# The second batch's activation blocks, moved out of the first step of attention and made in eight pieces

## The chip, the cores and the metric

The kernel runs on one core of a Trainium2 chip. The core has five engines that run side by side and meet at semaphores: TensorE (matrix products and transposes, PE in the profile), VectorE (DVE), ScalarE (ACT), GpSimd (POOL) and SyncE (SP), which here only issues transfers. Each engine takes its instructions in order. The metric is the time of one execution on the device in microseconds; a comparison goes by the median of several runs.

## The reference, cut to what matters

Two batches of 1024 tokens with 512 features go through a gated linear attention and then a feed-forward layer, each inside `x + layernorm(f(layernorm(x)))`.

```python
def _L0_attn_ref(hidden_states, qkv_w, out_w, gate_w, norm_w):   # 32 heads of 128
    qkv = silu(hidden_states @ qkv_w.T)             # q, k, v of each head
    ...
    # blocks of tokens, in order; kv is the state of a head
    scores = einsum(cq, ck) * diag_decay
    out    = scores @ cv + (cq * q_decay) @ kv
    kv     = kv * block_decay + (ck * k_decay).T @ cv
    ...
    xf = attn * rsqrt(mean(attn * attn) + EPS)
    return (sigmoid(hidden_states @ gate_w.T) * norm_w * xf) @ out_w.T
def _L0_ffn_ref(x, gate_t, up_t, down_t, gate_s, up_s, down_s):  # integer weights with scales
    hidden = silu(x @ gate_w.T) * (x @ up_w.T)
    return hidden @ down_w.T
```

## The kernel before, in words

**Steps.** Attention takes 32 steps: 16 pairs of heads for batch 0 (steps 0 to 15), then the same 16 pairs for batch 1 (16 to 31). The feed-forward layer follows. Step w is written as `first_window` (step 0) or `window(w)` on each engine, and `window(w)` also finishes pair a = w - 1: its attention, its gating and its share of the output projection, which VectorE adds into `y` (`add_out`).

**Products.** In a step the normalised activations are multiplied with the pair's weights of four kinds: k, q, v and the gate (KK, QQ, VV, GG). Each kind is a 2 by 2 block product done as seven products by Strassen's scheme in Winograd's form. The seven activation factors (B_11, B_21, B_22 and the combinations T_1 to T_4) lie in `xb`, seven blocks that stay for a whole batch; the weight factors are made anew for each kind (`combine_weights` on GpSimd). `product(w, kind, i)` is factor product i; I write KK5 for product 5 of kind KK. Every number is split in a high and a low half (`_hi` by ScalarE, `_lo` by a subtraction on GpSimd or VectorE), and a product is six matmuls of 128 x 512. The results are put together on VectorE (`keep_s2`, `keep_s3`, `finish_22`, `finish_12`, `finish_21`) and go through silu or sigmoid on ScalarE (`activate`).

**Attention of a pair.** VectorE turns k in two halves (`turn_k`), SyncE writes it to HBM and reads it back token by token (`k_write`, `k_read`), ScalarE applies the decay (`k_decay`). v goes the same way (`v_write`, `v_read`, then `turn_v`). GpSimd makes `query_decay`. TensorE runs `scores`, `contributions` and `attend`; VectorE runs `decay_scores`, `update_state` and `gate`.

**Both batches' blocks.** `xb` of batch 0 is made before and in step 0. Batch 1's blocks are also made in step 0: SyncE loads segments 2 and 3 of x into `y` (free until step 1), VectorE and ScalarE normalise them, TensorE turns them in eight fills of four transposes (`second_batch_fill`), ScalarE keeps them (`keep_second`), VectorE forms the combinations (`combine_second`), and the seven blocks in two halves each go through a ring of three buffers (`stage_hi`, `stage_lo` in turn on VectorE and GpSimd, `stage_write`) into the HBM tensor `x_blocks`, 14 writes of 512 KB in rows of 2 KB. `stages_out` makes VectorE, ScalarE and GpSimd wait for the last writes, since the buffers lie over tensors that step 1 uses. In step 15 SyncE loads the blocks into `xb`, each behind the last product that reads the old one (`activations`).

**Other work that fills steps.** In steps 2 to 15 ScalarE's queue loads the integer weights 128 x 512 at a time, three a step, into `tile_a`, and VectorE looks for the largest (`look_at_ints`, `look_at_block`). In steps 17 to 25 batch 0's output is normalised and turned for the feed-forward layer, one tile of 128 tokens a step: `load_tile`, `add_tile`, `statistics_of`, `tile_root`, `scales_of`, `normalise_tile`, `turn_tile` (four transposes), `tile_hi`, `tile_lo`, `store_tile`. I call 17 to 25 the tile steps.

The order on VectorE around the place where a piece's work is put, `window(w)`:

```python
gate(a, 0, 1)
if finish is not None:
    tile_lo(finish)
turn_k(w, 1, 0)
turn_k(w, 1, 1)
if checks is not None:
    look_at_block(checks, 0)
update_state(a, 1, 0)
keep_s3(w, QQ)
```

Of the kernel before, what the change touches and what calls it, by code (L numbers as in the profile page):

```python
# [6 lines left out]
P = 128  # L7
# [42 lines left out]
WIDTH_CHECKS = 3 * FF * HID // (P * HID)  # L50
# [68 lines left out]
def sandwich_kernel(nc, x, w_attn, w_out, norm_w, tables, w_ints, ffn_scales, down_s, out):  # L119
    ctx = ExitStack()  # L120
    with ctx:
# [15 lines left out]
        tile_stats = sb("tile_stats", [P, 6])  # L137
        tile_meanvar = sb("tile_meanvar", [P, 2])
        tile_var = sb("tile_var", [P, 1])
        tile_stdev = sb("tile_stdev", [P, 1])  # L140
        tile_rstd = sb("tile_rstd", [P, 1])
        tile_shift = sb("tile_shift", [P, 1])
        rms_term = sb("rms_term", [P, TILES])
        block_max = sb("block_max", [P, CHECKS_PER_WINDOW])
        ints_max = sb("ints_max", [P, CHECKS_PER_WINDOW])
        part_max = sb("part_max", [P, 1])
        all_max = sb("all_max", [P, 1])
# [15 lines left out]
        x_in = [None] + [sem(f"x_in{s}") for s in range(1, NSEG)]  # L163
# [7 lines left out]
        stage_hi_done = sem("stage_hi_done")  # L171
        stage_lo_dve, stage_lo_pool = sem("stage_lo_dve"), sem("stage_lo_pool")
        stage_out = [sem(f"stage_out{j}") for j in range(3)]
# [66 lines left out]
        tile_b = sb("tile_b", [P, HID], scope=two)  # L240
        v_tok = sb("v_tok", [P, QUADS, 2, CH, QUAD], scope=two)
        tile_a = sb("tile_a", [P, HID], scope=two)
# [6 lines left out]
        state = sb("state", [P, 2, CH, HD], scope=two)  # L249
# [10 lines left out]
        check = tile_a[:, :].bitcast(I32)  # L260
# [9 lines left out]
        sb("below_state", [P, 2 * SEQ], scope=one)  # L270
        xf1 = sb("xf1", [P, HALVES, 2, SEG], scope=one)
        tt1 = sb("tt1", [P, 4, SEG], scope=one)
        stage = sb("stage", [P, 3, 2, SEG], F32R, one)
# [37 lines left out]
        w_blocks = w_ints.rearrange("(c p n) -> c p n", p=P, n=HID)  # L311
        x_tiles = x.rearrange("(s t p) h -> s p t h", t=CH, p=P)
        x_rows = x.rearrange("(t p) h -> t p h", p=P)
        out_tiles = out.rearrange("(s t p) h -> s p t h", t=CH, p=P)
# [31 lines left out]
        norm_a = [NSEG + s for s in range(NSEG)]  # L346
        norm_b = [None, None, 2 * NSEG, 2 * NSEG + 1]
        norm_c = [2 * NSEG + 2 + s for s in range(NSEG)]
# [4 lines left out]

        def stages_out(eng):

            for j in range(3):
                eng.wait_ge(stage_out[j], 16 * ((2 * NB - j + 2) // 3))

        @block.sync
        def _(sp):  # L360
# [46 lines left out]
            def activations(b, i):  # L407

                sp.wait_ge(proj_done, products_until(PAIRS - 1, GG, i))
                sp.dma_start(xb[:, b].bitcast(F32), x_blocks[b]).then_inc(xb_in[b], 16)  # L410

            def stage_write(j):

                i, b = j // NB, j % NB
                if j % 2 == 0:
                    sp.wait_ge(stage_lo_dve, j // 2 + 1)
                else:
                    sp.wait_ge(stage_lo_pool, j // 2 + 1)
                sp.dma_start(x_blocks[b, :, :, i], stage[:, j % 3].bitcast(F32)).then_inc(stage_out[j % 3], 16)
# [48 lines left out]
            def first_window():  # L468
                for s in (2, 3):
                    sp.wait_ge(xt_done, BT)  # L470
                    sp.dma_start(y[:, tiles_of(s)], x_tiles[s]).then_inc(x_in[s], 16)
# [6 lines left out]
                for j in range(3):  # L478
                    stage_write(j)
                k_read(0, 0)  # L480
                weights(1, QQ, 1)
                stage_write(3)
                stage_write(4)
                v_write(0, 1)
                v_write(0, 0)
                stage_write(5)
                v_read(0, 0)
                weights(1, VV, 1)
                stage_write(6)
                v_read(0, 1)  # L490
                pair_table(1, 1)
                for j in range(NB, 2 * NB):
                    stage_write(j)
# [4 lines left out]
            sp.dma_start(y[:, tiles_of(1)], x_tiles[1]).then_inc(x_in[1], 16)  # L498
# [58 lines left out]
        def _(pool):  # L557
# [68 lines left out]
            def window(w, first=False, next_weights=True, rms_of=None, tile=None):  # L626
# [40 lines left out]
            def stage_lo(j):  # L667

                b = j % NB
                if b in (B_11, B_21, B_22):  # L670
                    src = xf1[:, int(b == B_22), int(b != B_11)]
                else:
                    src = tt1[:, (T_2, T_3, T_1, T_4).index(b)]
                pool.wait_ge(stage_hi_done, j + 1)
                pool.tensor_tensor(stage[:, j % 3, 1], src, stage[:, j % 3, 0].bitcast(F32),  # L675
                                   ALU.subtract).then_inc(stage_lo_pool, 1)

            def first_window():
# [8 lines left out]
                stage_lo(1)  # L687
                split_lo_s(0, GG)
                split_lo_a(0, GG)
                stage_lo(3)  # L690
                combine_weights(1, KK)
                stage_lo(5)
# [5 lines left out]
                stage_lo(7)  # L698
                stage_lo(9)
                split_lo_s(1, QQ)  # L700
                split_lo_a(1, QQ)
                stage_lo(11)
                stage_lo(13)
                stages_out(pool)
# [50 lines left out]
            window(1, first=True)  # L755
            with pool.Fori(2, PAIRS - 1) as w:
                window(w)
# [64 lines left out]
        def _(act):  # L822
# [43 lines left out]
            def keep_second(f):  # L866

                i, u = f // 4, f % 4
                act.wait_ge(xt_done, BT + f + 1)
                if f == 4:  # L870
                    act.wait_ge(t_done, 2 * 4)
                    act.wait_ge(stage_lo_dve, 4)
                    act.wait_ge(stage_lo_pool, 3)
                act.activation(xf1[:, u // 2, :, (u % 2) * 2 * P:(u % 2 + 1) * 2 * P],
                               yp[f % 2][:, :].rearrange("p (k n) -> p k n", k=2),
                               ACT.Copy).then_inc(xf_done, 1)

            def stage_hi(j):

                i, b = j // NB, j % NB  # L880
                if b in (B_11, B_21, B_22):
                    act.wait_ge(xf_done, BT + 4 * (i + 1))
                    src = xf1[:, int(b == B_22), int(b != B_11)]
                else:
                    act.wait_ge(t_done, 4 * (i + 1) + t_order.index(b) + 1)
                    src = tt1[:, (T_2, T_3, T_1, T_4).index(b)]
                wait(act, stage_out[j % 3], 16 * (j // 3))
                act.activation(stage[:, j % 3, 0], src, ACT.Copy).then_inc(stage_hi_done, 1)

# [20 lines left out]
            def split_out_hi(a):  # L910
                if isinstance(a, int) and a == 0:
                    stages_out(act)
# [55 lines left out]
            def look_at_ints(c):  # L968
                act.wait_ge(max_done, c + 1)
                act.dma_start(check[:, :], w_blocks[c]).then_inc(check_in, 16)  # L970
# [24 lines left out]
            def tile_root(i):  # L995

                act.wait_ge(tile_step, 5 * i + 3)
                act.activation(tile_stdev[:, :], tile_var[:, :], ACT.Sqrt).then_inc(tile_sd_ready, 1)
# [20 lines left out]

            def ffn_convert(n):  # L1020
# [9 lines left out]
            def window(w, next_weights=True, checks=None, first_done=False, finish=None, begin=None,  # L1030
                       into_ffn=False):
# [7 lines left out]
                if finish is not None:  # L1039
                    tile_root(finish)  # L1040
                activate(w, KK, OUT11)
                keep_s1(w, QQ)
                split_out_hi(a)
                if finish is not None:
                    normalise_tile(finish)
                split_hi_s(w, VV)
# [6 lines left out]
                if finish is not None:  # L1053
                    tile_hi(finish)
                square(a, 0, 1)
# [10 lines left out]
                if finish is not None:  # L1066
                    store_tile(finish)
                k_decay(w, 1, 0)
                k_decay(w, 1, 1)
# [11 lines left out]
                if checks is not None:  # L1081
                    look_at_ints(checks + 2)
                if begin is not None:
# [29 lines left out]
            def first_window():  # L1113
# [7 lines left out]
                square_root(2)  # L1121
                normalise(y_tile(2), y_tile(2), 2)
                keep_second(0)
                keep_second(1)
# [4 lines left out]
                square_root(3)  # L1129
                normalise(y_tile(3), y_tile(3), 3)  # L1130
                activate(0, KK, OUT21)
                keep_second(2)
                keep_second(3)
# [3 lines left out]
                stage_hi(0)  # L1137
                stage_hi(1)
                stage_hi(2)
# [6 lines left out]
                stage_hi(3)  # L1146
                activate(0, VV, OUT11)
                stage_hi(4)
                keep_s1(0, GG)
                activate(0, VV, OUT22)  # L1150
                stage_hi(5)
# [6 lines left out]
                stage_hi(6)  # L1158
                keep_second(4)
                keep_second(5)  # L1160
                activate(0, GG, OUT11)
                keep_second(6)
                keep_second(7)
                activate(0, GG, OUT22)
                for j in range(NB, NB + 3):
                    stage_hi(j)
# [1190 lines left out]
```

## Time and profile before

| what | value |
|---|---|
| median of 3 runs | 2441.73 us (2439.56 to 2442.05) |
| profiled execution, its own time | 2444.16 us |
| its span | 2442.4 us |
| TensorE busy, of the span | 2357.6 us (97%) |
| GpSimd busy | 1685.1 us (69%) |
| VectorE busy | 1406.8 us (58%) |
| ScalarE busy | 1190.5 us (49%) |

The span is the time from the first to the last instruction on the core. Busy time counts an engine's own work; an engine that isn't busy waits for another, and the idle time in front of an instruction is given in brackets with what ended it.

### The profile page before, as it was taken

What the parts mean: (1) busy time and instruction counts of PE and PEld (TensorE: products, weight loads), DVE (VectorE), ACT (ScalarE), POOL (GpSimd) and SP (SyncE); (2) the same over time, 40 slices, a digit from 0 to 9 for tenths busy, and PEclk for the clock granted to TensorE, in tenths of its full rate; (3) what the DMA queues carried; (4) which work ended last, traced back from release to release, by engine and by line L of the source; (5) the groups of instructions that cost most, each with busy time, mean ns of one, the idle gap of its engine ahead of it and who ended that gap; (6) DMA issues with size and microseconds to landing.
All of it is one profiled execution on the core that took longest, in us unless ns stands there. A gap on an engine that the chain in (4) does not pass through costs nothing.

```text
span 2442.4 us, 38239 instructions
## 1 busy us (share of the span) xinstructions
PE 2357.6 (97%) x12256; PEld 2011.5 (82%) x12256; DVE 1406.8 (58%) x2479; ACT 1190.5 (49%) x1719; POOL 1685.1 (69%) x1331
## 2 busy tenths in 40 slices
PE   4799999999999999999999999999999999899996
PEld 3588888888888888878888888888888888788885
DVE  5456665666666565656555555555555555465655
ACT  6544444444444444435555444444444444366563
POOL 4567777777777777767777777777777776474674
PEclk7899999999999999999999999999999999999998
DMA  3634444344344443363444444443333334512222
GB/s 108 211 118 125 129 128 122 123 125 125 118 126 129 129 128 122 125 232 116 149 130 129 136 137 137 137 138 126 112 110 110 113 110 139 178 61 70 78 66 90
DMA packets 156936, 304.94 MB, mean 125 GB/s; under 512 B 22464, under 2 KB 88000, under 8 KB 154176
## 3 DMA queue, kind: packets, MB, share of 16 engines
q1 hardware_dynamic: 143856, 279.37, 36.1%
q10 hardware_dynamic: 13008, 24.65, 2.9%
q8 instruction: 41, 0.67, 0.1%
q14 instruction: 31, 0.25, 0.0%
HBM read 216.92 MB, written 87.03 MB: 124 GB/s over the span
## 4 chain that ended last, share of the span: by engine, by line
PE 87%; POOL 3%; DMA 3%; DVE 3%; ACT 2%; issue 1%; SPq 0%; DVEq 0%; ACTq 0%; POOLq 0%
PE proj L1938 53%; PE yp L1938 17%; PE sc L2004 5%; PE sc L1981 4%; PE sc L2007 4%; PE sc L1994 4%; DMA fraw<-w_ints 1%; DMA v_tok<-v_blocks 1%; POOL f_lo L715 1%; DVE stats L1340 1%; DMA nw<-norm_w 0%; DMA fs_stage<-ffn_scales 0%; ACT y L831 0%; POOL stage L675 0%; POOL h_lo L725 0%
## 5 line engine op out<-in xcount | busy, mean ns | idle before, releaser
L1938 PE MATMUL proj<-xb,w_odd 128*128 128x512 f32 x2688 | 709.3, 402 | 17.9 <-POOL w_odd L579 13.0
L1938 PE MATMUL proj<-xb,w_even 128*128 128x512 f32 x2688 | 683.0, 397 | 16.2 <-DMA xb<-x_blocks 3.9
L1938 PEld LDWEIGHTS proj<-xb,w_even 128*128 128x128 f32 x2688 | 499.7, 190 | 118.5 <-issue 8.4
L1938 PEld LDWEIGHTS proj<-xb,w_odd 128*128 128x128 f32 x2688 | 492.7, 190 | 112.9 <-POOL w_odd L579 13.9
L601 POOL TENSOR_TENSOR qd<-q,table 128x512 f32<-128x512 f32 x128 | 164.5, 1298 | 218.2 <-ACT q L947 218.2
L1529 DVE TENSOR_TENSOR g<-sc,g 128x512 f32<-128x512 f32 x128 | 88.5, 691 | 269.6 <-ACT sq L961 269.5
L592 POOL TENSOR_TENSOR ow_lo<-v_tok,ow_hi 128x1024 fp32r<-128x1024 f32 x32 | 76.4, 2388 | 235.7 <-ACT ow_hi L915 235.7
L1536 DVE TENSOR_TENSOR y<-yp,y 128x512 f32<-128x512 f32 x240 | 164.6, 686 | 109.3 <-PE yp L1938 108.1
L1938 PE MATMUL proj<-x_t,f_hi 128*128 128x512 f32 x896 | 213.8, 391 | 2.5 <-issue 2.5
L586 POOL TENSOR_TENSOR w_odd<-ws,w_odd 128x1024 fp32r<-128x1024 f32 x64 | 153.6, 2400 | 73.6 <-ACT w_odd L907 73.6
L1938 PE MATMUL yp<-ow_hi,g_hi 128*128 128x512 f32 x512 | 202.5, 395 | 0.2 <-DVE y L1536 0.2
L1938 PEld LDWEIGHTS proj<-x_t,f_hi 128*128 128x128 f32 x896 | 168.9, 189 | 37.8 <-issue 2.6
L1938 PE MATMUL yp<-ow_hi,g_lo 128*128 128x512 f32 x512 | 199.5, 390 | 0.0
L1938 PE MATMUL yp<-ow_lo,g_hi 128*128 128x512 f32 x512 | 199.4, 389 | 0.0
L2004 PE MATMUL sc<-pd,v 128*128 128x128 f32 x1024 | 188.4, 276 | 3.3 <-DVE state L1521 3.3
L2007 PE MATMUL sc<-qd,state 128*128 128x128 f32 x896 | 174.1, 276 | 0.0
L2004 PEld LDWEIGHTS sc<-pd,v 128*128 128x128 f32 x1024 | 160.9, 193 | 13.8 <-issue 3.7
L617 POOL TENSOR_TENSOR g_lo<-g,g_hi 128x512 fp32r<-128x512 f32 x128 | 163.4, 1299 | 9.5 <-ACT g_hi L966 9.5
L586 POOL TENSOR_TENSOR w_even<-ws,w_even 128x1024 fp32r<-128x1024 f32 x64 | 153.7, 2401 | 16.9 <-ACT w_even L907 16.9
L613 POOL TENSOR_TENSOR sumsq<-sumsq,sq 128x512 f32<-128x512 f32 x124 | 160.9, 1297 | 4.7
L725 POOL TENSOR_TENSOR h_lo<-hid,h_hi 128x512 fp32r<-128x512 f32 x56 | 73.2, 1309 | 118.7 <-ACT h_hi L1239 118.7
L954 ACT ACTIVATE kd<-k_tok,table 128x512 f32<-128x512 f32 x128 | 85.5, 715 | 128.9 <-DMA k_tok<-k_blocks 128.9
(169 smaller groups left out, 4411.3 us busy)
## 6 DMA issues: line engine op xcount, KB each, us to landing
raw<-w_attn SPq DMA_DIRECT2D x128, 512.0 KB, 3.7
k_blocks<-pd SPq DMA_DIRECT2D x64, 512.0 KB, 3.6
k_tok<-k_blocks SPq DMA_DIRECT2D x256, 128.0 KB, 2.9
v_blocks<-vf SPq DMA_DIRECT2D x64, 512.0 KB, 2.7
v_tok<-v_blocks SPq DMA_DIRECT2D x256, 128.0 KB, 3.0
v_tok<-w_out SPq DMA_DIRECT2D x32, 512.0 KB, 4.5
fraw<-w_ints SPq DMA_DIRECT2D x13, 1024.0 KB, 5.0
tile_a<-w_ints ACTq DMA_DIRECT2D x42, 256.0 KB, 3.5
```

The costliest lines, as they stand in the source:

```text
L586: pool.tensor_tensor(w_lo[slot][:, S_1:S_4 + 1], ws[:, :, :, :], w_hi[slot][:, S_1:S_4 + 1].bitcast(F32), ALU.subtract).then_inc(wlo_s_don ...
L601: pool.tensor_tensor(qd[:, s, h].rearrange("p (c n) -> p c n", c=CH), q[:, h, half(s)].rearrange("p (c n) -> p c n", c=CH), decay.unsqueez ...
L613: pool.tensor_tensor(total, total, sq[:, h], ALU.add).then_inc(ss_done, 1)
L617: pool.tensor_tensor(g_lo[:, h], g[:, h, half(s)], g_hi[:, h].bitcast(F32), ALU.subtract).then_inc(glo_done, 1)
L954: act.activation(kd[:, s, h].rearrange("p c (i d) -> p i c d", i=QUADS), k_tok[:, :, h], ACT.Copy, scale=table[:, TAB_K + h:TAB_K + h + 1] ...
L1529: dve.tensor_tensor(at, sc[h][:, :], at, ALU.mult).then_inc(gated_done, 1)
L1536: dve.tensor_tensor(y[:, t], yp[t % 2][:, :], y[:, t], ALU.add).then_inc(yacc_done, 1)
L1938: last = pe.matmul(psum, s, m, start=start and n == 0, stop=n == len(terms) - 1, skip_group_check=more)
L1981: last = pe.matmul(sc[h][:, chunk(c)], k[:, h, tok], q[:, h, tok], start=True, stop=True)
L1994: last = pe.matmul(sc[h][:, chunk(c)], kd[:, s, h, c], v[:, s, c, h], start=True, stop=True)
L2004: last = pe.matmul(sc[h][:, chunk(c)], v[:, s, c, h], pd[:, s, h, c], start=True, stop=not inter)
L2007: last = pe.matmul(sc[h][:, chunk(c)], state[:, h, (c - 1) % CH], qd[:, s, h, chunk(c)], start=False, stop=True)
```

## The change

Batch 1's blocks leave step 0 altogether: the loads, statistics, fills, `combine_second`, `stage_hi`, `stage_lo`, `stage_write` and `stages_out` are gone. Instead a piece of 2 x 128 tokens and half of the features is made in each of steps 1 to 8. At the end of step w - 1 ScalarE's queue loads two tiles of x (`load_piece`) and VectorE takes their statistics. In step w they are normalised, turned by four transposes, combined by four subtractions of 128 columns, split, and both halves are written to `x_blocks` from ScalarE's queue, 448 KB each in rows of 512 bytes. The buffer `piece` lies where no other tensor does, so `state` moves in SBUF. The tiles are loaded and normalised twice, once for either half of the features. The looks at the integer weights become 21 of 128 x 1024, in steps 9 to 15, and use the same buffer.

In `window(w)` ScalarE has `piece_root` behind `keep_s1(w, KK)`, `normalise_piece` behind `split_out_hi(a)`, `keep_piece` behind `activate(w, KK, OUT21)`, `piece_high` ahead of `k_decay(w, 1, 0)` and `store_high` behind it, and `store_low` and the next `load_piece` behind `gated_hi(a, 1, 1)`. VectorE has `scales_of_piece` behind `update_state(a, 0, 1)`. The diff, cut:

```diff
-WIDTH_CHECKS = 3 * FF * HID // (P * HID)
+WIDTH_CHECKS = 3 * FF * HID // (2 * P * HID)
...
+        piece = sb("piece", [P, 2 * NB * P], scope=two)
...
+        tiles = piece[:, 0:2 * HID].rearrange("p (t n) -> p t n", t=2)
+        piece_hi = piece[:, 0:NB * P].bitcast(F32R)
+        piece_lo = piece[:, NB * P:2 * NB * P]
+        mix = piece_lo.rearrange("p (b n) -> p b n", b=NB)
...
@@ GpSimd, window @@
                 add_squares(a, 1, 0, first)
+                if part is not None:
+                    split_piece(part)
...
+            def split_piece(j):
+                pool.wait_ge(piece_hi_done, j + 1)
+                pool.tensor_tensor(piece_lo.bitcast(F32R), piece_lo, piece_hi.bitcast(F32),
+                                   ALU.subtract).then_inc(piece_lo_done, 1)
...
@@ ScalarE @@
+            def load_piece(j, u):
+                wait(act, piece_hi_out, 16 * j)
+                for s in range(HALVES):
+                    act.dma_start(tiles[:, s], x_pairs[u, HALVES + s]).then_inc(piece_in[s], 16)
+            def piece_root(j):
+                act.wait_ge(piece_step, 7 * j + 5)
+                act.activation(tile_stdev[:, :], tile_var[:, :], ACT.Sqrt).then_inc(piece_sd_ready, 1)
+            def normalise_piece(j):
+                act.wait_ge(piece_step, 7 * j + 7)
+                for s in range(HALVES):
+                    act.activation(tiles[:, s], tiles[:, s], ACT.Identity, bias=tile_shift[:, s:s + 1],
+                                   scale=tile_rstd[:, s:s + 1]).then_inc(piece_normed, 1)
+            def keep_piece(j):
+                act.wait_ge(piece_turned, j + 1)
+                wait(act, piece_lo_out, 16 * j)
+                for m in range(2):
+                    act.activation(mix[:, B_21 * m:B_21 * m + T_3 + 1:T_3],
+                                   yp[0][:, 2 * P * m:2 * P * (m + 1)].rearrange("p (s n) -> p s n", s=HALVES),
+                                   ACT.Copy).then_inc(piece_kept, 1)
+            def piece_high(j):
+                act.wait_ge(piece_mixed, 4 * (j + 1))
+                act.activation(piece_hi, piece_lo, ACT.Copy).then_inc(piece_hi_done, 1)
...
@@ VectorE @@
+            def statistics_of_piece(j, n):
+                for s in range(HALVES):
+                    dve.wait_ge(piece_in[s], 16 * (j + 1))
+                    dve.bn_stats(tile_stats[:, s], tiles[:, s]).then_inc(piece_step, 1)
+                dve.wait_ge(piece_step, 7 * j + 2)
+                keep_b(n)
+                for s in range(HALVES):
+                    dve.bn_aggr(tile_meanvar[:, s], tile_stats[:, s]).then_inc(piece_step, 1)
...
+            def mix_piece(j):
+                dve.wait_ge(piece_kept, 2 * (j + 1))
+                dve.tensor_tensor(mix[:, T_1], mix[:, T_3], mix[:, B_11], ALU.subtract).then_inc(piece_mixed, 1)
+                dve.wait_ge(piece_mixed, 4 * j + 1)
+                dve.tensor_tensor(mix[:, T_2], mix[:, B_22], mix[:, T_1], ALU.subtract).then_inc(piece_mixed, 1)
+                dve.tensor_tensor(mix[:, T_3], mix[:, B_22], mix[:, T_3], ALU.subtract).then_inc(piece_mixed, 1)
+                dve.wait_ge(piece_mixed, 4 * j + 2)
+                dve.tensor_tensor(mix[:, T_4], mix[:, B_21], mix[:, T_2], ALU.subtract).then_inc(piece_mixed, 1)
...
@@ VectorE, window @@
                 gate(a, 0, 1)
                 if finish is not None:
                     tile_lo(finish)
+                if part is not None:
+                    mix_piece(part)
                 turn_k(w, 1, 0)
...
                     statistics_of(begin, w)
+                elif next_part:
+                    statistics_of_piece(w, w)
...
@@ VectorE, first_window @@
-                combine_second(0)
-                stage_lo(0)
...
                 turn_v(0, 1, 0)
                 turn_v(0, 1, 1)
-                stage_lo(10)
-                stage_lo(12)
+                statistics_of_piece(0, 0)
...
@@ TensorE, window, behind product(w, KK, 4) @@
+                if part is not None:
+                    turn_piece(a, part, a)
...
@@ TensorE, project_out(a, 0) @@
+                    if part is not None:
+                        pe.wait_ge(piece_kept, 2 * (a + 1))
```

## Rows read from the trace of the kernel before

**Rows 1.** The page's forty slices: TensorE's granted clock, in tenths.

```profile
PEclk7899999999999999999999999999999999999998
```

**Rows 2.** Stretches in us: busy time (count) of each engine, clock, DMA share, GB/s.

```profile
100.00:120.00 20.00, 12.35 (x51) 9.78 (x49) 13.89 (x18) 7.58 (x13) 9.96 (x7) 0.83 0.72 223
...
200.00:260.00 60.00, 60.00 (x322) 51.57 (x322) 37.51 (x65) 26.95 (x40) 42.79 (x36) 1.00 0.43 132
...
633.30:695.90 62.60, 62.60 (x337) 53.90 (x336) 38.23 (x67) 29.01 (x44) 45.48 (x37) 1.00 0.39 126
```

**Rows 3.** Timeline, TensorE, step 0 and the start of step 1.

```profile
44.51 2.90 PE L1938 MATMUL proj<-xb,w_even 128*128 128x512 f32 x6 [3.69 <-DVE k L1442]
...
85.26 2.93 PE L1938 MATMUL proj<-xb,w_odd 128*128 128x512 f32 x6 [6.37 <-POOL w_odd L579]
...
106.68 5.49 PE L1938 MATMUL proj<-xb,w_odd 128*128 128x512 f32 x12 [4.85 <-DVE g L1448]
111.96 2.97 PE L1938 MATMUL proj<-xb,w_even 128*128 128x512 f32 x12
...
131.35 1.06 PE L2004 MATMUL sc<-pd,v 128*128 128x128 f32 x4
```

**Rows 4.** Timeline, the other engines, step 0.

```profile
76.70 0.61 ACT L947 ACTIVATE q<-q 128x512 f32<-128x512 f32 x1
...
79.87 1.28 POOL L675 TENSOR_TENSOR stage<-tt,stage 128x512 fp32r<-128x512 f32 x1
...
93.27 0.61 ACT L947 ACTIVATE vf<-vf 128x512 f32<-128x512 f32 x1
...
101.61 1.30 DVE L1490 STREAM_TRANSPOSE v<-v_tok 128x512 f32<-128x512 f32 x2 [3.88 <-DMA v_tok<-v_blocks]
...
102.84 0.65 DVE L1388 TENSOR_TENSOR tt<-xf 128x512 f32<-128x512 f32 x1
...
105.94 0.68 DVE L1448 TENSOR_TENSOR g<-proj,g 128x512 f32<-128x512 f32 x1
```

**Rows 5.** The page's DMA issues: count, KB each, median us to landing.

```profile
k_blocks<-pd SPq DMA_DIRECT2D x64, 512.0 KB, 3.6
...
tile_a<-w_ints ACTq DMA_DIRECT2D x42, 256.0 KB, 3.5
```

**Rows 6.** One tile, ow_hi on ScalarE: once a step; steps 2 and 14.

```profile
L915 ACT ACTIVATE ow_hi<-v_tok x1: 1049/1049/1049, 193.9 to 193.9; 128x1024 fp32r<-128x1024 f32 x1
...
L915 ACT ACTIVATE ow_hi<-v_tok x1: 1049/1049/1049, 945.9 to 945.9; 128x1024 fp32r<-128x1024 f32 x1
```

**Rows 7.** One tile, tile_b on TensorE: ns min/median/max, first and last start.

```profile
L2117 PE MATMUL yp<-ident,tile_b x32: 272/272/273, 1211.2 to 1653.5; 128*128 128x128 f32 x32
```

**Rows 8.** Timeline, four engines, step 19, a tile step.

```profile
1271.71 0.80 ACT L1003 ACTIVATE tile_b<-tile_a,tile_shift,tile_rstd 128x512 f32<-128x512 f32 x1
...
1278.71 0.69 DVE L1529 TENSOR_TENSOR g<-sc,g 128x512 f32<-128x512 f32 x1 [1.53 <-ACT sq L961]
...
1279.92 1.29 DVE L1482 STREAM_TRANSPOSE pd<-k 128x512 f32<-128x512 f32 x2
1281.50 1.11 DVE L1521 SCALAR_TENSOR_TENSOR state<-state,b_prev,sc 128x128 f32<-128x128 f32 x3 [0.28 <-PE sc L1994]
1282.79 0.69 DVE L1448 TENSOR_TENSOR q<-proj,q 128x512 f32<-128x512 f32 x1 [0.18 <-PE proj L1938]
...
1280.15 1.28 POOL L617 TENSOR_TENSOR g_lo<-g,g_hi 128x512 fp32r<-128x512 f32 x1 [0.32 <-ACT g_hi L966]
...
1284.56 1.64 PE L1938 MATMUL proj<-xb,w_odd 128*128 128x512 f32 x6
```

**Rows 9.** One tile (ints_max on VectorE), then timelines around 673 us.

```profile
L1544 DVE TENSOR_TENSOR ints_max<-ints_max,block_max x42: 159/298/1889, 203.8 to 1049.5; 128x1 f32<-128x1 f32 x42
...
672.69 2.41 POOL L586 TENSOR_TENSOR w_even<-ws,w_even 128x1024 fp32r<-128x1024 f32 x1
...
673.40 1.72 DVE L1544 TENSOR_TENSOR ints_max<-ints_max,block_max 128x1 f32<-128x1 f32 x1
```

More of the change, by code:

```diff
@@ L162, in sandwich_kernel @@
         x_first_in = [sem(f"x_first_in{t}") for t in range(CH)]
-        x_in = [None] + [sem(f"x_in{s}") for s in range(1, NSEG)]
+        x_in = sem("x_in")
         const_done, ln_own = sem("const_done"), sem("ln_own")
@@ L239, in sandwich_kernel @@
         k_tok = sb("k_tok", [P, QUADS, 2, CH, QUAD], scope=two)
[L240 removed]
         v_tok = sb("v_tok", [P, QUADS, 2, CH, QUAD], scope=two)
[L242 removed]
+        state = sb("state", [P, 2, CH, HD], scope=two)
         q = sb("q", [P, 2, SEQ], scope=two)
@@ L624, in add_tile, with window @@
                 pool.tensor_tensor(tile_a[:, :], tile_a[:, :], tile_b[:, :], ALU.add).then_inc(tile_added, 1)
-            def window(w, first=False, next_weights=True, rms_of=None, tile=None):
+            def window(w, first=False, next_weights=True, rms_of=None, tile=None, part=None):
                 a = w - 1
@@ L754, in _ @@
             first_window()
-            window(1, first=True)
-            with pool.Fori(2, PAIRS - 1) as w:
+            window(1, first=True, part=0)
+            with pool.Fori(2, 2 * CH + 1) as w:
+                window(w, part=w - 1)
+            with pool.Fori(2 * CH + 1, PAIRS - 1) as w:
                 window(w)
@@ L1067, in window @@
                     store_tile(finish)
+                if part is not None:
+                    piece_high(part)
                 k_decay(w, 1, 0)
+                if part is not None:
+                    store_high(part)
                 k_decay(w, 1, 1)
@@ L1082, in window @@
                     look_at_ints(checks + 2)
+                if part is not None:
+                    store_low(part)
+                if next_part is not None:
+                    load_piece(w, next_part)
                 if begin is not None:
@@ L1170, in first_window @@
                 activate(0, GG, OUT21)
-                for j in range(NB + 3, 2 * NB):
-                    stage_hi(j)
+                load_piece(0, 0)
             square_root(0)
@@ L1510, in update_state @@
                 if s == 0 and h == 0:
-                    if isinstance(a, int) and a == 0:
-                        stages_out(dve)
                     dve.wait_ge(b_kept, a + 1)
@@ L1603, in window @@
                     scales_of(finish)
+                if part is not None:
+                    scales_of_piece(part)
                 keep_s3(w, KK)
@@ L1613, in window @@
                     tile_lo(finish)
+                if part is not None:
+                    mix_piece(part)
                 turn_k(w, 1, 0)
@@ L2009, in attend, with project_out @@
                 last.then_inc(attn_done, 1)
-            def project_out(a, t, tile=None, downs=0):
+            def project_out(a, t, tile=None, downs=0, part=None):
                 if t == 0:
@@ L2015, in project_out @@
                         pe.wait_ge(tile_lo_done, tile + 1)
+                    if part is not None:
+                        pe.wait_ge(piece_kept, 2 * (a + 1))
                 if t % CH == 0:
@@ L2118, in turn_tile, with turn_piece, window @@
                 last.then_inc(tile_turned, 1)
-            def window(w, x_wait=False, rms_of=None, tile=None):
+            def turn_piece(a, i, j):
+                pe.wait_ge(piece_normed, 2 * (j + 1))
+                wait(pe, yacc_done, BT * a - 1)
+                for m in range(2):
+                    for s in range(HALVES):
+                        last = pe.transpose(yp[0][:, chunk(2 * m + s)], tiles[:, s, chunk(2 * m + i)],
+                                            ident[:, :])
+                last.then_inc(piece_turned, 1)
+            def window(w, x_wait=False, rms_of=None, tile=None, part=None):
                 a = w - 1
@@ L2136, in window @@
                     turn_tile(a, tile)
+                if part is not None:
+                    turn_piece(a, part, a)
                 product(w, QQ, 6)
@@ L2147, in window @@
                     pe.wait_ge(rms_ready, rms_of + 1)
-                project_out(a, 0, tile)
+                project_out(a, 0, tile, part=part)
                 product(w, QQ, 4)
```

254 lines of the change are left out of this document (82 added, 172 removed).

## Prediction

> **What bounds the kernel now.** I read the page's forty slices first: TensorE's granted clock is below nine tenths only in the first two and the last of them [rows 1]. The stretches then split the run in two. From 200 us on TensorE is busy 60.00 of 60 us at full clock; from 100 to 120 us it is busy 12.35 of 20 [rows 2]. So a step is bound by TensorE everywhere except at the start, and this change touches both kinds of place: it takes work out of step 0, where TensorE waits for others, and puts it into steps 1 to 8, where TensorE waits for nobody. The profiled execution took 2444.16 us, 1.76 us more than its span; the median of the runs is 2.43 us below it, so I work out differences and subtract them from 2441.73.
>
> **The saving in step 0.** I rebuild the chain of step 0 without the removed work and ask when TensorE would start `attend(0, 0, 0)`, which it now does at 131.35 us [rows 3]. Up to the product KK5 at 44.51 us nothing changes.
> - KK5 takes about 2.8 us at the lower clock. `keep_s3` (0.7) then frees KK3 at 48.0; it also runs at the lower clock and ends near 50.7. Eight more products at 1.38 us each (a pair takes 2.97 with overlap [rows 3]) bring 61.7. Fills and normalisations between them are gone. `finish_12` of QQ stands behind `turn_k(0, 0)`, which waits for the landing of `k_write(0, 1)`; that write is now queued behind the load of step 1's KK weights, released near 56.1. Issue at 56.6 plus 3.6 to 4.5 (median landing 3.6 [rows 5]) plus two transposes gives 63.0 for VV7, a wait of 1.3. ScalarE's last silu of QQ then starts near 65.3.
> - From that silu (76.70) to GG1 (85.26) takes 8.56 now, through GpSimd's two query decays, one `stage_lo` of 1.2 us and two weight splits [rows 3, 4]. Without the `stage_lo` it is 7.3: GG1 at 72.6. TensorE is done at 67.1 and idles 5.5 us; GpSimd, not the activation work, sets this stretch.
> - GG1 to the last silu of VV: 8.0 (85.26 to 93.27), kept: 80.6. From there to `turn_v` 8.34 (93.27 to 101.61), the round trip of v through HBM, kept: 89.0. `turn_v` to GG3 is 5.07 (101.61 to 106.68), of which the four additions of `combine_second` from 102.84 to `decay_scores` take 2.5; 2.6 stay: GG3 at 91.6. From GG3 to KK1 of step 1 is 5.28 (106.68 to 111.96): 96.9. Step 1 starts 15.1 us earlier.
> - From KK1 to `attend(0, 0, 0)` takes 19.4 now, with waits in it (KK2, KK3) that come from `stages_out` and the late `stage_hi`. Run without waits it is seven products and two contributions, 11.3. New in front of it: `statistics_of_piece(0)` makes VectorE wait for two loads that ScalarE issues at about 98.0 and 98.4 (landing 3.5 later, as loads of the same size do [rows 5]). Statistics end near 103.3, `keep_s2` at 104, the two state updates, `scales_of_piece` and `keep_s3` at 107.8, so KK3 waits about 1.1: `attend` at 109.7 with some slow clock.
>
> Saving: 131.35 - 109.7 = 21.7 us. Bounds: three waits stay (1.3, 5.5 and about 4.3 before GG3), and each may cost the clock again (2.90 for six products after one, 5.49 for twelve after another, against 2.97 for twelve). If the cold stretches add up, 18; if v's round trip shortens without the 14 `stage_write`s, 25.
>
> **The cost of a piece, TensorE.** Four transposes a step. Batch 1's tile steps have the same four: their marks lie 442.3 us apart over seven steps and three transposes of 0.11 [rows 7], 63.13 a step, against (945.9 - 193.9) / 12 = 62.67 for batch 0's steps [rows 6]. So 0.46 each, 8 x 0.46 = 3.7 us.
>
> **The cost of a piece, VectorE's queue.** This is the disputed term. I lay the piece over the tile step around 1280 us [rows 8]. ScalarE's normalisation is two activations instead of one, 0.7 more, so `gate(a, 0, 1)` moves from 1278.71 to about 1279.6 and is out at 1280.2. There `mix_piece` takes the place of `tile_lo`. Behind it in the same queue stand two transposes, three state updates and `keep_s3`, from 1279.92 to 1281.50 to 1282.79: at least 3.06 us of work once `mix_piece` is out, and product QQ3 (1284.56) waits for the last. So `mix_piece` may end at 1281.5 without any cost. Its four subtractions of 128 columns are about 0.28 each (between 0.16 for one column [rows 9] and 0.65 for 512 [rows 4]), 1.0 in all: 1281.2, just in time.
>
> But they read two operands from SBUF, and such an operation doesn't run beside GpSimd's. The third look of a check step adds one column to another; the fastest of its kind takes 0.159 us, this one runs from 673.40 to 675.12, which is where GpSimd's split from 672.69 ends [rows 9]. In the piece step GpSimd is at `gated_lo(a, 0, 0)` when the mix begins, and takes `gated_lo(a, 0, 1)` (1.28 us [rows 8]) 0.8 us after the gate, amid the four. The dependent steps of the mix leave it a gap. One such block: the mix ends at 1282.7, QQ3 waits 1.2. Two: 1284.0 and 2.5. None: 0. I take one, since the request falls between the second and third subtraction: 8 x 1.2 = 9.6 us.
>
> The Trainium skill's "SBUF — State Buffer", section "Who interferes with whom", says that an operation with two SBUF inputs contends with a reading GpSimd operation and that whoever comes first has the shared pair for the whole instruction. By that rule all four could be blocked in the worst case, 4 x 1.28 = 5.1 us a step, 41 us in all; the rows here show the block for a single operation and not who wins when both wait. This rule speaks against the change more than anything else I found.
>
> **The rest.** `statistics_of_piece` is 0.7 longer than the tile's; `turn_v` behind it still waits for its load. `split_piece` (896 columns, about 2.1 us on GpSimd by 2.41 for 1024 [rows 9]) delays the low halves that `project_out(4)` and `keep_s1(GG)` want; GpSimd is idle for 17.1 of 62.6 us of a step [rows 2], and what is late there I take as covered. `piece_high` and `store_high` lie in ScalarE's wait for k. The writes go out in 512-byte runs; no row of this kernel prices them alone, so between nothing and 0.5 a step, taken as nothing because the DMA engines are busy 0.39 of a step [rows 2]. The looks at the integers become 21 of 1024 columns in steps 9 to 15 instead of 42 of 512 in 2 to 15: 0.6 longer each; the first one of a step stands in front of QQ3 with about 0.7 of room after a block, so 0 to 0.5 x 7, taken as 0.3 in all. The change of batch (step 16) isn't touched.
>
> **Sum.** -21.7 + 3.7 + 9.6 + 0.3 = -8.1 us: 2433.6 us.
>
> **Rivals.**
> - No block in the mix: -21.7 + 3.7 = -18.0, 2423.7 us. For: there are 1.3 us of room and 1.0 of work. Against: the row at 673.40 and GpSimd's place. Chance 0.30.
> - Two blocks: +20 instead of +9.6, 2444.0 us, no change that can be told. Chance 0.16.
> - Slower: three blocks, 3.8 us before QQ3 in each of eight steps, 30.4 + 3.7 - 21.7 = +12.4, 2454 us. It decides from 2.25 us a step on (18.0 / 8); over 2.9 it is slower by more than 0.2%. For: VectorE and GpSimd alternate if both always have a request. Against: GpSimd is between two operations when the mix starts. Chance 0.12.
> - Step 0 doesn't shorten as said, since its two long waits are GpSimd's splits and v's round trip and neither is removed: if only half is saved (11), the result is +2.6, 2444 us. Against: `stage_lo`, `combine_second` and `stages_out` stand on the chain themselves. Chance 0.07.
>
> **How the numbers follow.** About 0.2% (4.9 us) is what a measurement of this kernel can tell from no change. The forecast has 0.35, with its own range 2428 to 2438. Faster: 0.35 + 0.30 + a little of the last = 0.67. Same: 0.16 + the rest of the last and some overlap = 0.20. Slower 0.13. The range takes in no block with a good step 0 (-21.7) and two blocks with a little more (+4.3): 2420 to 2446.
>
> **What would show it.** In the trace after: `attend(0, 0, 0)` near 110 us (18 to 25 earlier); GG1 still waits for GpSimd, GG3 for VectorE; steps of batch 0 with a piece 64.3 us apart by the mark of `ow_hi` (63.1 if the mix isn't blocked, 65.6 if blocked twice), with TensorE's idle time before the product that follows `keep_s3` of q; some of the mix's subtractions near 1.3 us instead of 0.28; steps 9 to 15 at 62.7. I am wrong if piece steps wait elsewhere (k's round trip, a GpSimd half) or if steps 9 to 15 lengthen.

## The result, and the profile after

The kernel after takes 2446.71 us (median of 20 runs, 2441.72 to 2450.3) against 2442.41 us for the kernel before on the same chips (20 runs, 2439.56 to 2448.47). The ratio is 1.0016 (95% interval 1.001 to 1.0022): 4.3 us slower where the forecast was 8.1 us faster. That is inside the 0.2% which counts as no change, and 0.7 us above the upper end of the range (2446). The profiled execution took 2447.89 us with a span of 2445.7 us.

TensorE's timeline of the kernel after, step 0 and the start of step 1:

```profile
45.26 2.90 PE L1932 MATMUL proj<-xb,w_even 128*128 128x512 f32 x6 [4.17 <-DVE k L1412]
...
64.87 4.42 PE L1932 MATMUL proj<-xb,w_even 128*128 128x512 f32 x18 [1.10 <-DVE q L1433]
...
74.40 2.93 PE L1932 MATMUL proj<-xb,w_odd 128*128 128x512 f32 x6 [5.11 <-POOL w_odd L562]
...
92.89 5.43 PE L1932 MATMUL proj<-xb,w_odd 128*128 128x512 f32 x12 [3.57 <-DVE g L1418]
98.16 2.92 PE L1932 MATMUL proj<-xb,w_even 128*128 128x512 f32 x12
...
108.73 1.65 PE L1932 MATMUL proj<-xb,w_even 128*128 128x512 f32 x6 [0.39 <-DVE k L1418]
110.22 0.61 PE L1998 MATMUL sc<-pd,v 128*128 128x128 f32 x4
```

The products are those of [rows 3]: GG1 comes at 74.40 instead of 85.26, GG3 at 92.89 instead of 106.68, `attend(0, 0, 0)` of step 1 at 110.22 instead of 131.35. Up to `attend`, 21.1 us are gained, and the same two waits stay, for GpSimd's weight split and for VectorE's g. So the loss is behind this point. Stretches between the marks of `ow_hi` (start of one to start of the next; its length, TensorE busy and its count, granted clock, DMA share, GB/s), steps 1, 2, 5 and 7, and the first one without a piece:

```profile
111.39:176.43 65.04, 62.75 (x332) 1.00 0.41 132
176.43:243.29 66.86, 64.45 (x339) 0.97 0.40 128
...
374.24:440.95 66.71, 64.21 (x343) 1.00 0.40 128
...
506.35:571.89 65.54, 63.52 (x343) 1.00 0.40 130
...
636.91:699.58 62.67, 62.67 (x338) 1.00 0.43 139
```

Steps without a piece stay at the 62.67 us of [rows 6]. The eight with one take (636.91 - 111.39) / 8 = 65.69 us, almost the 65.6 that the prediction gave for a mix that is blocked twice. TensorE, which waited for nobody in these steps before [rows 2], now isn't busy for about 2.2 us of each. Its waits from 105 to 640 us (total, times, longest):

```profile
PE proj L1932 <- DVE q L1418: 16.5, 8, 2.5
PE proj L1932 <- DVE k L1418: 0.9, 2, 0.5
PE proj L1932 <- ACT g L879: 0.3, 1, 0.3
PE yp L2100 <- ACT piece L984: 0.2, 1, 0.2
```

The first line is the product that the prediction named: QQ3 waits for `keep_s3` of q in every piece step. Step 7, timelines of VectorE, GpSimd and TensorE, which answer to [rows 8]:

```profile
515.08 0.69 DVE L1497 TENSOR_TENSOR g<-sc,g 128x512 f32<-128x512 f32 x1 [2.30 <-ACT sq L909]
515.69 0.62 DVE L1582 TENSOR_TENSOR piece<-piece 128x128 f32<-128x128 f32 x1
516.34 0.29 DVE L1584 TENSOR_TENSOR piece<-piece 128x128 f32<-128x128 f32 x1
516.55 1.41 DVE L1585 TENSOR_TENSOR piece<-piece 128x128 f32<-128x128 f32 x1
517.88 1.37 DVE L1587 TENSOR_TENSOR piece<-piece 128x128 f32<-128x128 f32 x1
519.17 1.29 DVE L1452 STREAM_TRANSPOSE pd<-k 128x512 f32<-128x512 f32 x2
520.40 1.06 DVE L1489 SCALAR_TENSOR_TENSOR state<-state,b_prev,sc 128x128 f32<-128x128 f32 x3
521.38 0.68 DVE L1418 TENSOR_TENSOR q<-proj,q 128x512 f32<-128x512 f32 x1
...
514.86 1.29 POOL L600 TENSOR_TENSOR g_lo<-g,g_hi 128x512 fp32r<-128x512 f32 x1
516.51 1.29 POOL L600 TENSOR_TENSOR g_lo<-g,g_hi 128x512 fp32r<-128x512 f32 x1 [0.36 <-ACT g_hi L914]
517.76 2.75 POOL L596 TENSOR_TENSOR sumsq<-sumsq,sq 128x512 f32<-128x512 f32 x2
...
522.12 1.65 PE L1932 MATMUL proj<-xb,w_odd 128*128 128x512 f32 x6 [2.02 <-DVE q L1418]
```

Read the ends against each other. The first subtraction ends at 516.31, 0.16 behind GpSimd's first `g_lo` (516.15): it lost 0.33. The third is handed over at 516.55, 0.04 behind the start of the second `g_lo`, and ends at 517.96, 0.16 behind that one's end. GpSimd's `add_squares` follows at once, and the fourth ends at 519.25, 0.12 behind the middle of the two (517.76 + 2.75 / 2). The mix lasts 3.5 us (515.69 to 519.25); the prediction had 1.0 for it without a block and 2.5 with one. The other piece steps show the same four lengths, except that the fourth subtraction of step 1 took 0.69 us.

### The profile page after: what moved, and what is told of

Its sections match the earlier page's. It is cut to its first block, busy times and chain, and to the rows that moved or that the text cites. A ratio compares the mean times of both kernels' runs of the same rounds, so it can differ in the third digit from the quotient of the medians.

```text
span 2445.7 us, 38159 instructions
## 1 busy us (share of the span) xinstructions
PE 2356.5 (96%) x12256; PEld 2010.1 (82%) x12256; DVE 1407.2 (58%) x2488; ACT 1199.5 (49%) x1739; POOL 1691.5 (69%) x1332
## 4 chain that ended last, share of the span: by engine, by line
PE 82%; DMA 5%; DVE 5%; ACT 3%; issue 3%; POOL 1%; SPq 1%; DVEq 0%; ACTq 0%; POOLq 0%
PE proj L1932 50%; PE yp L1932 17%; PE sc L1975 4%; PE sc L1998 4%; PE sc L2001 4%; PE sc L1988 3%; DMA nw<-norm_w 2%; DMA v_tok<-v_blocks 1%; SPq L405 1%; DVE v L1460 1%; DVE pd L1452 0%; ACT k L895 0%; DMA k_blocks<-pd 0%; DMA k_tok<-k_blocks 0%; DVE piece L1587 0%
## 5 line engine op out<-in xcount | busy, mean ns | idle before, releaser
L1932 PE MATMUL proj<-xb,w_odd 128*128 128x512 f32 x2688 | 709.6, 402 | 32.7 <-DVE q L1418 16.5
L1489 DVE SCALAR_TENSOR_TENSOR state<-state,b_prev,sc 128x128 f32<-128x128 f32 x384 | 131.7, 343 | 21.2 <-PE sc L1988 9.8
```

What stands on the lines that cost most here:

```text
L1489: dve.scalar_tensor_tensor(state[:, h, c], state[:, h, (c - 1) % CH], b_prev[:, h:h + 1], new, ALU.mult, ALU.add).then_inc(state_done, 1)
L1932: last = pe.matmul(psum, s, m, start=start and n == 0, stop=n == len(terms) - 1, skip_group_check=more)
```

## The experiments

The first four start from the kernel after, the last four from the second of them ("One operand from PSUM"). Kernels of one group ran beside the same runs of before (2442.43 us for the first group, 2442.7 us for the second).

**Move the mix.** `mix_piece` goes from in front of `turn_k(w, 1, 0)` to behind `keep_s3(w, QQ)`:

```diff
-                if part is not None:
-                    mix_piece(part)
                 turn_k(w, 1, 0)
...
                 keep_s3(w, QQ)
+                if part is not None:
+                    mix_piece(part)
                 turn_k(w, 0, 0)
```

> Change: mix_piece(part) stands behind keep_s3(w, QQ) in VectorE's queue instead of in front of turn_k(w, 1, 0); all else as after. Theory A (what the piece costs is mostly that two of the four subtractions are blocked by GpSimd, so that the mix takes 3.5 us where 1.3 are free before product QQ3): QQ3's wait of 2.0 to 2.3 us a step goes, marks of ow_hi in piece steps 63.3 to 64.0 us apart instead of 65.8, time 2429.5 us (2427 to 2433), ratio to before 0.993 to 0.996. Rival B (the queue is late already when the mix begins, through the statistics before turn_v and the second normalising activation): QQ3 still waits 1 us or more, marks 64.8 or more apart, 2438 to 2443. Rival C (the stall is only moved, to finish_22 and turn_k(0, 0) behind the mix): QQ3 doesn't wait, but a later product does, 2436 to 2446.

Measured: 2427.08 us (5 runs, 2425.0 to 2430.11), ratio 0.9943 (0.9929 to 0.9957). The waits of TensorE from 105 to 640 us:

```profile
PE proj L1932 <- DVE q L1426: 2.3, 7, 0.6
PE yp L2100 <- ACT piece L984: 0.2, 1, 0.2
```

The 16.5 us are gone, and only 2.3 us come back at the next product that waits for q. Blocks still lengthen the subtractions in this place, three of the four; VectorE's timeline in step 7:

```profile
500.25 0.69 DVE L1418 TENSOR_TENSOR q<-proj,q 128x512 f32<-128x512 f32 x1 [0.19 <-PE proj L1932]
500.86 0.28 DVE L1582 TENSOR_TENSOR piece<-piece 128x128 f32<-128x128 f32 x1
501.18 1.33 DVE L1584 TENSOR_TENSOR piece<-piece 128x128 f32<-128x128 f32 x1
502.44 0.82 DVE L1585 TENSOR_TENSOR piece<-piece 128x128 f32<-128x128 f32 x1
503.18 0.82 DVE L1587 TENSOR_TENSOR piece<-piece 128x128 f32<-128x128 f32 x1
503.92 0.70 DVE L1452 STREAM_TRANSPOSE pd<-k 128x512 f32<-128x512 f32 x1
```

The mix takes 3.1 us here, but it now lies where VectorE would wait for k's round trip. Theory A holds; rival B (the queue is late anyway) doesn't, and rival C is worth the 2.3 us. The marks are 63.3 to 63.8 apart.

**One operand from PSUM.** The transposes' bank holds the same numbers as the copy in SBUF, so each subtraction takes its first operand from there:

```diff
-dve.tensor_tensor(mix[:, T_1], mix[:, T_3], mix[:, B_11], ALU.subtract)
+dve.tensor_tensor(mix[:, T_1], yp[0][:, P:2 * P], mix[:, B_11], ALU.subtract)
...
-dve.tensor_tensor(mix[:, T_4], mix[:, B_21], mix[:, T_2], ALU.subtract)
+dve.tensor_tensor(mix[:, T_4], yp[0][:, 2 * P:3 * P], mix[:, T_2], ALU.subtract)
...
-                        pe.wait_ge(piece_kept, 2 * (a + 1))
+                        pe.wait_ge(piece_mixed, 4 * (a + 1))
```

> Change: each of the four subtractions reads its first operand from the transposes' bank yp[0] instead of from the copy in SBUF, so that it has one SBUF input; same place, same count, same semaphores, and project_out(0) waits for the mix instead of for the copy. Theory A (lock): each subtraction takes 0.25 to 0.4 us, none over 0.7; the mix is out about 1.3 us after the gate; QQ3 waits 0 to 0.3; marks 63.3 to 64.0 apart; 2429.5 us (2426 to 2433). Rival D (the mix costs by its work and its chained semaphores, not by the lock): the mix still takes 2.5 us or more, QQ3 waits 1.2 or more, 2440 to 2447.

Measured: 2424.45 us (5 runs, 2422.56 to 2426.47), ratio 0.9926 (0.9913 to 0.994). VectorE's timeline in step 5:

```profile
371.79 0.69 DVE L1497 TENSOR_TENSOR g<-sc,g 128x512 f32<-128x512 f32 x1 [2.31 <-ACT sq L909]
372.40 0.28 DVE L1582 TENSOR_TENSOR piece<-yp,piece 128x128 f32<-128x128 f32 x1
372.71 0.29 DVE L1584 TENSOR_TENSOR piece<-yp,piece 128x128 f32<-128x128 f32 x1
372.92 0.28 DVE L1585 TENSOR_TENSOR piece<-yp,piece 128x128 f32<-128x128 f32 x1
373.12 0.28 DVE L1587 TENSOR_TENSOR piece<-yp,piece 128x128 f32<-128x128 f32 x1
...
375.52 0.68 DVE L1418 TENSOR_TENSOR q<-proj,q 128x512 f32<-128x512 f32 x1
```

Same place, same count, same chain of semaphores on VectorE, and the mix takes 1.0 us instead of 3.5; QQ3 no longer waits. What differs for the subtractions is the memory of one operand, so the block needs the second operand in SBUF. The time is 18.0 us under the kernel before and below the range that I had expected (2426 to 2433). It has the lowest median here, but its interval overlaps those of the moved mix, of both repairs together and of the doubled stores. The forecast for a mix without a block was 18.0 us as well; that it fits to the tenth is luck, since at the mark of step 9 the lead is 15.8 us (616.80 against 632.59) and the rest comes later.

**GpSimd yields once.**

```diff
                 gated_lo(a, 0, 1)
+                if part is not None:
+                    pool.wait_ge(piece_mixed, 4 * (part + 1))
                 add_squares(a, 0, 0, first)
```

> Change: GpSimd waits for the fourth subtraction before add_squares(a, 0, 0), one wait more in its queue; nothing else. Theory A (the third subtraction is blocked by the second gated_lo, the fourth by add_squares): the third stays at 1.4 us, the fourth falls from 1.37 to 0.29; QQ3 waits 1.0 to 1.3 instead of 2.0 to 2.3; marks 64.7 apart; 2438 us (2436 to 2441). That is the single block that the prediction had. Rival D (work, not the lock): no change, 2445 to 2448. A rival to both: GpSimd, later by 0.5 us, delays w_lo or g_lo and TensorE waits there; over 2448.

Measured: 2436.51 us (11 runs, 2431.79 to 2440.1), ratio 0.9977 (0.9968 to 0.9986). TensorE's wait for q, then VectorE and GpSimd in step 2:

```profile
PE proj L1934 <- DVE q L1420: 9.8, 8, 1.6
```

```profile
185.68 0.60 DVE L1584 TENSOR_TENSOR piece<-piece 128x128 f32<-128x128 f32 x1
186.32 0.29 DVE L1586 TENSOR_TENSOR piece<-piece 128x128 f32<-128x128 f32 x1
186.53 0.28 DVE L1587 TENSOR_TENSOR piece<-piece 128x128 f32<-128x128 f32 x1
186.73 1.38 DVE L1589 TENSOR_TENSOR piece<-piece 128x128 f32<-128x128 f32 x1
...
186.51 1.46 POOL L600 TENSOR_TENSOR g_lo<-g,g_hi 128x512 fp32r<-128x512 f32 x1 [0.37 <-ACT g_hi L916]
```

With one long block instead of two the wait is 9.8 us for the eight steps, close to what the prediction reckoned (9.6; in single steps it is 0.87 to 1.58). The time is then 5.9 us under the kernel before, inside the range of the forecast (2428 to 2438) but short of its 8.1. I had expected the block always at the third subtraction. In steps 2 and 7 the third went ahead (0.28, and `g_lo` took 1.46 instead of 1.29), and the fourth was blocked instead: 1.38. The mean of the third is 1.13, of the fourth 0.56. It is one long block in either case.

**Statistics later.**

```diff
-                elif next_part:
-                    statistics_of_piece(w, w)
...
                 turn_v(w, 0, 1)
+                if next_part:
+                    statistics_of_piece(w, w)
```

> Change: statistics_of_piece(w, w), with its keep_b, stands behind turn_v(w, 0, 1) and not before turn_v(w, 0, 0). Theory A: the late output weights move ScalarE's ow_hi by no more than 0.2 us, since it stands behind keep_s1 of q there, and QQ3's wait stays at 2.0 or more; 2443.5 to 2447. Rival B (the queue is late through the statistics): v_tok and the output weights come some 2 us earlier, the mix begins 0.5 us or more earlier, QQ3's wait falls by as much, 2439 to 2443.

Measured: 2444.73 us (11 runs, 2441.73 to 2447.38), ratio 1.0005 (0.9996 to 1.0014). QQ3 waits 14.6 us in all instead of 16.5, and the waits for k are gone. That lies between the two expectations: QQ3's wait fell by 0.24 us a step, where rival B wanted 0.5. From `attend(0, 0, 0)` to the mark of step 9 this trace takes 525.0 us, the one of the kernel after 526.7. So the waits show a small part of the late queue in the loss, not the main one; the times don't show it, since the intervals of the two kernels overlap.

**Both repairs together.** The second and fourth edit in one kernel.

> Change: the subtractions with a PSUM operand and the statistics behind turn_v, both together. If the small waits for keep_s3 of k (0.8 us in two steps) come from the statistics in front of turn_v: they go, 2422.5 us (2421 to 2424.5), 1 to 3 us under the kernel with the PSUM operands alone. Rival: the two edits overlap and nothing is left to gain, 2424.5.

Measured: 2426.42 us (6 runs, 2423.52 to 2428.74), ratio 0.9933 (0.9921 to 0.9945): not better than the PSUM operands alone, whose interval it overlaps, and not the 2422.5 that I had hoped for. The waits for k that VectorE released are gone, but near the end of step 5 TensorE now waits 0.9 us for ScalarE's k; what makes it wait in just that step stays open.

**Transposes twice.**

```diff
-                for m in range(2):
+                for m in (0, 1, 0, 1):
```

> Change: to the kernel with the PSUM operands, each of the four transposes is made twice (eight a step). If TensorE's queue is the bound in the piece steps and a transpose costs 0.115 us there: 8 x 0.46 = 3.7 us more, 2428.2 us (2426.5 to 2430), marks 0.46 further apart. If the transposes lie in time that TensorE has to spare, or cost by their latency (0.60 us for the four in the record): 2424.5, or 2430 and more.

Measured: 2428.37 us (5 runs, 2427.44 to 2429.34), ratio 0.9942 (0.9929 to 0.9955), 3.9 us more than with four. The intervals overlap a little, and the kernel with doubled stores, which ran beside this one, is only 2.4 us faster. The marks are the better evidence: without steps 1 and 5 they are 63.4 to 63.6 apart (63.53 in the mean) against 62.8 to 63.2 (63.00), 0.5 more for four more transposes, which agrees with the 0.46 of the prediction. Over all eight steps the difference is smaller, 1.9 us from `attend(0, 0, 0)` to the mark of step 9, since step 5, with its wait for k, is longer with four than with eight (64.75 against 63.69).

**A long mix without a lock.** Twelve more subtractions in front of the four:

```diff
+                for n in range(12):
+                    if n == 6:
+                        dve.wait_ge(extra, 12 * j + 6)
+                    dve.tensor_tensor(piece[:, (n % 6) * P:(n % 6 + 1) * P], yp[0][:, P:2 * P], mix[:, B_11],
+                                      ALU.subtract).then_inc(extra, 1)
```

> Change: to the kernel with the PSUM operands, twelve more subtractions of the same form (one PSUM, one SBUF operand, 128 columns) in front of the four; they write where the high part goes later. No lock is involved, and the mix gets about as long as in the changed kernel: 0.95 + 12 x 0.21 = 3.5 us. If all of the changed kernel's loss is the length of the mix (its wait before QQ3 and what the clock takes after such a wait): QQ3 waits 1.9 to 2.1 us in each of eight steps, 2446 us (2442 to 2449). If a part of the 22 us between the two kernels is what the lock does to GpSimd: QQ3 waits the same, but the time is 2424.5 + 15 to 16 = 2440 us (2438 to 2442).

Measured: 2447.5 us (11 runs, 2444.65 to 2450.26), ratio 1.0023 (1.0015 to 1.0032). VectorE in step 7, then TensorE's wait:

```profile
515.84 2.59 DVE L1586 TENSOR_TENSOR piece<-yp,piece 128x128 f32<-128x128 f32 x12
518.35 0.28 DVE L1588 TENSOR_TENSOR piece<-yp,piece 128x128 f32<-128x128 f32 x1
...
519.07 0.28 DVE L1593 TENSOR_TENSOR piece<-yp,piece 128x128 f32<-128x128 f32 x1
```

```profile
PE proj L1938 <- DVE q L1419: 16.1, 8, 2.6
```

A mix of 3.5 us made of short, free operations gives the wait of the kernel after (16.1 and 16.5 us) and its time (ratios 1.0023 and 1.0016 to the kernel before, with overlapping intervals). So what the blocks cost is the length that they give to the mix in that place; a further cost, through GpSimd's side, doesn't show.

**Stores twice.** Both stores of a piece are issued a second time, to a spare tensor:

```diff
+                act.dma_start(spare[0, j], piece_hi.bitcast(F32).rearrange("p (b n) -> p b n", b=NB)).then_inc(piece_hi_twice, 16)
                 act.dma_start(piece_blocks[0, j],
...
+                act.dma_start(spare[1, j], mix[:, :, :]).then_inc(piece_lo_twice, 16)
                 act.dma_start(piece_blocks[1, j], mix[:, :, :]).then_inc(piece_lo_out, 16)
```

> Change: to the kernel with the PSUM operands, each store of a piece (high and low part, 128 partitions, 512-byte runs) is issued a second time, to a spare tensor. If the stores are hidden, as the prediction took: 2424.5 us (2423 to 2426). If they are not: up to 0.5 us a step, 2428.5.

Measured: 2425.97 us (5 runs, 2423.04 to 2427.56), ratio 0.9931 (0.9918 to 0.9944). The DMA share of a piece step rises from 0.42 to 0.48, and the time doesn't move by more than the intervals. Its mark of step 9 stands at 616.89 against 616.80. The stores are hidden.

## Why the prediction was wrong

- **The saving in step 0: right.** Forecast 21.7 us, measured 21.1 (131.35 to 110.22). The intermediate points came 0.5 to 1.9 us later than forecast: VV7 at 64.87 (63.0), GG1 at 74.40 (72.6), GG3 at 92.89 (91.6), KK1 at 98.16 (96.9), `attend` at 110.22 (109.7). The rival that step 0 doesn't shorten is out. That the total is so close is in part luck: `attend` starts at 109.4 to 112.1 us in eight of the nine traces with pieces and at 105.60 in the ninth, with the moved mix, whose edit doesn't touch step 0. There GG3 and its neighbour ran at full clock (granted 1.00, 3.01 us for the twelve matmuls), here at the lower level (0.52, 5.43 us), behind waits of nearly the same length (3.46 and 3.57 us).
- **The transposes: right** as far as the runs tell. 3.7 us were forecast; doubling them added 0.5 us to a quiet step, 3.9 us to the median.
- **The mix: this step failed.** Mechanism, place and product were right (`mix_piece` blocked by GpSimd, QQ3 waits for `keep_s3` of q). The sum took one block of 1.2 us a step, 9.6 us; the trace shows two long ones and a third of 0.33 us, and the wait is 16.5 us, 2.06 a step. The room in front of QQ3 was as forecast, some 1.4 us (1.3); the length of the mix was not, 3.5 us (2.5). The prediction laid only `gated_lo(a, 0, 1)` over the mix. It left out what stands behind that in GpSimd's queue: `add_squares(a, 0, 0)`, which starts the moment `gated_lo` is done, and also the end of `gated_lo(a, 0, 0)`, which cost the first subtraction its 0.33. The prediction's argument against more blocks, that GpSimd is between two operations when the mix starts, goes against its own reading two paragraphs earlier and against the trace: `gated_lo(a, 0, 0)` runs until 0.46 us after that start. With `add_squares` held back, the wait was the forecast one (9.8 us). The rival with two blocks (2444.0 us, chance 0.16) is what happened; it gave their wait as 20 us, the wait was 16.5. That 65.69 us a step came so close to its 65.6 is partly luck: the wait was 0.4 shorter, and other terms made up for it.
- **What follows a wait: left out.** From `attend(0, 0, 0)` to the mark of step 9 the kernel before takes 501.2 us (131.35 to 632.59) and the kernel after 526.7 (110.22 to 636.91), 25.5 more. QQ3's waits are 16.5 of it, the transposes 3.7, the small waits for k, g and the piece 1.4 (0.9 + 0.3 + 0.2), and 3.9 are left. Part of that is the clock: behind the wait of step 2, matmuls for `yp` took 0.62 us, though 0.39 is their record at full clock.

```profile
192.20 1.71 PE L1932 MATMUL proj<-xb,w_odd 128*128 128x512 f32 x6 [2.41 <-DVE q L1418]
193.71 0.62 PE L1932 MATMUL yp<-ow_hi,g_hi 128*128 128x512 f32 x1
...
196.26 1.95 PE L1932 MATMUL proj<-xb,w_odd 128*128 128x512 f32 x6
198.05 0.38 PE L1998 MATMUL sc<-pd,v 128*128 128x128 f32 x2
```

  The stretch from 194 to 197, with the same columns as [rows 2]:

```profile
194.00:197.00 3.00, 3.00 (x8) 2.35 (x8) 2.93 (x7) 1.47 (x2) 0.00 (x0) 0.50 0.81 243
```

  That is the lower of the two levels, and it is the only such fall in the piece steps of this trace; it takes away about 1.7 us (3.4 us at half clock). The other 2.2 were not settled. Between kernels that differ in the mix alone, from `attend(0, 0, 0)` to the mark of step 9: with the PSUM operands it takes 506.7 us, with 9.8 us of waits for q (GpSimd yields) 518.3, and with 16.5 us (the kernel after) 526.7. So the waits cost 11.6 and 20.0 us, some 1.2 times their length; the traces of the first two have no fall of the clock there. The long mix without a lock says the same: 16.1 us of waits, 527.0 us, with two falls. In the medians the kernel after is 22.3 us above the one with PSUM operands (2446.71 - 2424.45); what exceeds 20.0 isn't found in the piece steps.
- **Stores, checks, `split_piece`: nothing of them shows.** Stores twice change nothing. The marks of steps 9 to 15 stay 62.7 us apart, so the wider looks are hidden (the sum had 0.3 for them). `split_piece` was not tried alone, but in the piece steps TensorE waits for nothing that GpSimd made.
- **The skill's rule.** The Trainium skill ("SBUF — State Buffer", "Who interferes with whom") says that a VectorE operation with two SBUF inputs contends with a reading GpSimd operation and that the first to come holds the pair of SBUF ports that they share for its whole length. The traces agree: three subtractions of 0.28 us ended 0.12 to 0.16 us behind a GpSimd operation, and with one operand in PSUM none was longer than 0.29. The worst case that the prediction worked out from it, four full blocks, didn't come: the first subtraction met only the last 0.46 us of a GpSimd operation, and the second fell into a gap of 0.36 us. The kernel before had a hint: `tile_lo`, which the mix replaced in the overlay on the tile step, reads one of its operands from `yp`, and it takes 0.68 us every time, so its place said nothing on two SBUF operands.

The sum at the mark of step 9: -21.1 + 16.5 + 3.7 + 1.4 + 3.9 = +4.4 us, where 3.9 is a remainder and no measurement of its own; the marks say +4.3 (636.91 against 632.59). What follows differs by a microsecond or two from trace to trace, and the spans end at +3.3 (2445.7 against 2442.4), the medians at +4.3.

## What to carry to other kernels

When a short VectorE operation with two SBUF operands is put into a queue, lay GpSimd's queue beside it for as long as the *blocked* sequence would last, not the free one: each block makes room for the next operation of GpSimd, and four operations of 0.28 us became 3.5 us. If one of the operands is also in PSUM, take it from there; if not, put the group behind what TensorE waits for in that queue, where VectorE itself would wait: here the one was worth 22 us and the other about 20, which the intervals don't tell apart. And where TensorE is the bound, reckon a new wait at more than its length: here it was 1.2 times, with clock falls in some traces.

## What was not expected of the hardware

- Where VectorE and GpSimd both kept asking, they took turns: the third and the fourth subtraction each got through between two GpSimd operations, and GpSimd's own records were at most 0.17 us longer for it (`g_lo` 1.46 instead of 1.29 where the third subtraction went ahead; two `sumsq` 2.75 where the kernel with the PSUM operands has 2.72). Here the short operation paid for the long one, hardly the other way round.
- Who comes first can't be read from the starts: the third subtraction that starts at 516.55, 0.04 us behind `g_lo`, was blocked, and the one that starts at 186.53 (with GpSimd yielding), 0.02 behind it, was not.
- The length of a wait alone doesn't tell whether the clock falls behind it. In the piece steps it fell to 0.50 behind waits of 2.41 us (kernel after, step 2), 2.50 (statistics later, step 5), and 2.40 and 1.78 (long mix, steps 3 and 5), for 3 to 4 us each time. It stayed at full level behind waits of 2.49 us (kernel after, step 4) and 2.60 (long mix, step 1).
